# Four indirect gathers in flight instead of two, in the attention layer of a fused four-layer GNN kernel

## The reference

```python
h_in  = _attention_aggregate(h_proj, src, dst, a_in, n)
h_out = _attention_aggregate(h_proj, dst, src, a_out, n)
# inside, for each edge and each of 4 heads:
e = leaky_relu(score(sender) + score(receiver)); e_max = segment_max(e, receiver)
alpha = exp(e - e_max[receiver]); alpha = alpha / (segment_sum(alpha)[receiver] + 1e-8)
return segment_sum(h_proj[sender] * alpha, receiver)
```

## Time and profile before

| | us |
|---|---|
| median of 3 runs | 3679.42 (3669.36 to 3679.49) |
| the profiled execution | 3675.2 |
| its span, first to last instruction | 3673.1 |
| mean granted TensorE clock | 0.786 of full speed |

### The profile page before, as it was taken

The page is one execution under the profiler, slowest core; times in us unless marked ns, Lnnn a source line. Parts: engine busy times, 40 slices in busy tenths (PEclk is TensorE's granted clock), DMA queues, the critical chain, the costliest instruction groups (busy, mean ns, idle before and its releaser), DMA issues.

```text
span 3673.1 us, 46525 instructions
## 1 busy us (share of the span) xinstructions
PE 2217.1 (60%) x12603; PEld 1303.9 (35%) x12659; DVE 2275.1 (62%) x3122; ACT 834.8 (23%) x1389; POOL 1652.6 (45%) x1455
## 2 busy tenths in 40 slices
PE   0688777778968999857333333334557554336663
PEld 0333545544534555524311111112456211115563
DVE  8999888885497003532233334337577896349877
ACT  0198333320012001120000100002334221004442
POOL 7300333330477777740266666657644666630000
PEclk9799999999979999979555555555589897555797
DMA  2000111114434342044433333332367333320352
GB/s 65 0 0 0 45 45 45 45 40 135 125 108 117 87 100 42 1 96 102 67 90 89 91 93 90 90 86 74 88 206 232 101 88 96 88 48 0 107 176 85
DMA packets 195114, 301.51 MB, mean 82 GB/s; under 512 B 120540, under 2 KB 133818, under 8 KB 194922
## 3 DMA queue, kind: packets, MB, share of 16 engines
q1 hardware_dynamic: 138986, 175.88, 15.1%
q0 software_dynamic: 40512, 62.87, 9.2%
q10 hardware_dynamic: 15552, 61.94, 5.6%
HBM read 191.65 MB, written 88.01 MB: 76 GB/s over the span
## 4 chain that ended last, share of the span: by engine, by line
PE 28%; DMA 24%; issue 17%; DVE 15%; POOL 9%; ACT 5%; ACTq 0%; DVEq 0%; SPq 0%; POOLq 0%; PEldq 0%
DMA arena<-T_att,idx 23%; PE PS L537 10%; POOL arena L1304 9%; PE PS L698 6%; PE PS L883 6%; ACT arena L513 3%; DVE arena L558 3%; PE PS L972 3%; DVE arena L1195 1%; DVE arena L373 1%; PE PS L475 1%; DVE arena L489 1%; PE PS L959 1%; DMA T_att<-parts 0%; DVE arena L566 0%
## 5 line engine op out<-in xcount | busy, mean ns | idle before, releaser
L1304 POOL DMA_INDIRECT arena<-T_att,idx x864 | 843.2, 976 | 627.8 <-DMA arena<-T_att,idx 457.5
L537 PE MATMUL PS<-arena 128*128 128x400 f16 (+2 forms) x4320 | 781.0, 331 | 266.1 <-issue 106.0
L1139 DVE TENSOR_REDUCE arena<-PS 128x1024 f32 (+1 forms) x432 | 504.7, 1216 | 582.5 <-PE PS L1106 562.3
L537 PEld LDWEIGHTS PS<-arena 128*128 128x128 f16 (+2 forms) x4320 | 528.3, 158 | 509.1 <-issue 350.0
L1477 POOL DMA_INDIRECT order<-arena x400 | 513.3, 1283 | 252.4 <-issue 252.4
L1095 PE MATMUL PS<-ident_b,score_buf 128*32 128x128 bf16 x864 | 96.2, 279 | 552.9 <-ACT score_buf L1068 542.0
L1106 PE MATMUL PS<-arena,pick 128*128 128x512 bf16 x812 | 340.5, 525 | 139.7 <-DVE arena L1139 107.1
L558 DVE TENSOR_SCALAR arena<-arena 128x1600 f16<-128x1600 f16 x448 | 381.1, 896 | 59.8 <-PE PS L537 55.6
L698 PE MATMUL PS<-arena 128*128 128x512 f16 (+1 forms) x1575 | 318.7, 362 | 95.5 <-issue 82.1
L632 POOL TENSOR_TENSOR rdeg<-rdeg,arena 128x1600 f32<-128x1600 f32 x48 | 160.1, 3337 | 307.0 <-ACT arena L616 307.0
L1095 PEld LDWEIGHTS PS<-ident_b,score_buf 128*32 128x32 bf16 x864 | 71.3, 124 | 625.3 <-issue 554.7
(11 more groups left out here) (258 smaller groups left out, 2797.6 us busy)
## 6 DMA issues: line engine op xcount, KB each, us to landing
spill<-arena SPq DMA_DIRECT2D x108, 560.0 KB
arena<-spill ACTq DMA_DIRECT2D x108, 560.0 KB
arena<-A SPq DMA_DIRECT2D x50, 800.0 KB
A<-arena SPq DMA_DIRECT2D x50, 400.0 KB, 2.4
arena<-A SPq DMA_DIRECT2D x50, 400.0 KB
arena<-T_att,idx POOLq DMA_INDIRECT x864
order<-arena POOLq DMA_INDIRECT x400
T_att<-h SPq DMA_DIRECT2D x2, 1600.0 KB, 13.9
```

The source lines that it names most:

```text
L537: return t.matmul(where, lhsT, rhs, start=False, stop=True, skip_group_check=True)
L1139: v.tensor_reduce(cmax[d][:, u:u + 2, bass.ds(i * SLOTS + half * GROUP + q // 2 * QUAD, QUAD)], PS[:, u * BANK:(u + 2) * BANK].rearrange(" ...
L1304: p.indirect_dma_start(out=ring1[:, b, j, :], out_offset=None, in_=T_att[d][:, :], in_offset=bass.IndirectOffsetOnAxis(ap=idx[:, d, k:k + ...
```

## The change

`FLYING` goes from 2 to 4, and each of the three buffers of `ring1` gets four landing semaphores instead of two. `PER`, the number of gathers of a group that share a semaphore, becomes 2 instead of 4. A gather then waits for the gather four places before it, where it waited for the one two places before. The keep and the spill wait for four semaphores where they waited for two. The number of gathers, their order, sizes and buffers stay as they are.

```diff
-        landed1 = [[sem(f"landed1_{b}_{q}") for q in range(2)] for b in range(RING1)]
+        landed1 = [[sem(f"landed1_{b}_{q}") for q in range(4)] for b in range(RING1)]
...
-        FLYING = 2
+        FLYING = 4
         PER = GROUP // FLYING
```

## The result

The changed kernel takes 3375.75 us (median of 4, 3372.55 to 3378.3) beside 3679.45 for the kernel before: a ratio of 0.9184, 95% interval 0.917 to 0.9199. The forecast was 3436, its low end 3405. The way it moved was forecast rightly, and so was the mechanism in POOL's stream; the gain was 60 us larger than forecast.

The account below looks back on a forecast made before the run. POOL's gathers, waiting for landings, were taken to bound top 0 and the end of top 1. Saving 110 us in top 0, losing 10 in guard 0 and weighted 0, saving 143 in top 1 gave 243 less: 3436 us, range 3405 to 3540.

Parts of the forecast that it names:

- 1.25 us between gathers, landings well inside four places: POOL's stream: gathers start 1.25 us apart; a landing's 2.84 us fits within four starts, 5.0 us.
- The step across the keep, 1.75 us: POOL, between groups: one step of 1.75 us beside seven of 1.25, making 10.5 us a group.
- The two additions of 0.20: POOL, per group: 0.13 us for pauses without a releaser, 0.07 for late landings beside spills, giving 10.7 us.
- The first 36 us of guard 0: Start of guard 0, during DVE's whole-row casts: more in flight doesn't help, 12 gathers as before.
- The rest of guard 0, 157 us: Guard 0 after its first 36 us: 153 us plus 4 for more gather groups disturbing it, 112 gathers.
- Weighted 0, +6 us, a gather each 1.63: Weighted 0: 6 us longer, 194 us, from a third more gathers; 119 gathers at 1.63 us each.
- What ends top 1: End of top 1: the later of DVE's reduces (3049) and the gathers (3045), so DVE at 3049, against 3291.8.
- The lower bound, 3405: Whole kernel: 10.5 us a group, no loss in guard 0 or weighted 0 gives 3414; clock luck, 3405.
- Rival 1: Gather stream: landings slow down when more are in flight; half the gain a group, 3533 us; chance 0.14.
- Rival 2: Gather queue: gathers don't overlap, one finishes every 1.6 us; within 10 us of 3679; chance 0.04.
- Rival 3: DMA rings: gathers delay the spill, so POOL waits for the third buffer; 3759 us; chance 0.04.
- Rival 4: Guard 0: the 3 us lost per gather group double, 40 us on the path, about 3476; chance 0.06.

Follow-up runs that it names:

- e13: The kernel before the change (two in flight), unaltered, run again for a trace of its own: 3665.55 us.
- e4: Changed kernel, but POOL issues no gather from group 54 on until weighted 0 and its output are done: 4082.77 us.
- e2: Changed kernel with a small memset on POOL after each gather, so most gathers start 1.41 us apart: 3729.47 us.
- e7: Changed kernel with four gathers in flight in direction 0 but only two in direction 1: 3615.07 us, ratio 0.9876.
- e5: Changed kernel unaltered, run again in a later set: 4087.44 us, ratio 1.1177 to the kernel before.
- e12: Changed kernel unaltered, run once more in another set: 3361.67 us, ratio 0.9202 to the kernel before.
- e10: Changed kernel with SP's spill waiting for POOL's keep instead of the four landings: 3365.99 us, ratio 0.9213.

## Why the prediction was wrong, point by point

- **1.25 us between gathers, landings well inside four places:** right. 229.1 us of POOL's 323.1 idle are now "issue".
- **The step across the keep, 1.75 us:** a mis-sized term. It measured 1.38, so a group is 7 x 1.25 + 1.38 = 10.13, where the text had 10.5. The 0.53 us of idle time behind the cast were read as the price of a keep. With four in flight they are 0.16, so the rest probably was an unmarked wait for the landing two places back (in e13, again two in flight, it is 0.49 to 0.63 in a quiet stretch). The two additions of 0.20 came to 0.12: 556 us for 434 gathers is 10.25 a group. Over 54 groups the 0.45 that the forecast had too much is 24 us. Top 0 itself: 577 forecast, 564 measured, its gathers starting 4.5 us later than in before (1813.1 for 1808.6).
- **The first 36 us of guard 0:** right, 14 gathers for 12.
- **The rest of guard 0, 157 us:** the larger of the two mis-sized terms, 102.7 measured. The text took the 40 us over guard 1's length for a property of the stream ("the stage itself is disturbed by the stream") and carried it over. It was a property of the set of runs from which the trace came, as e13 shows for the kernel before: with the same two-deep stream beside it the stretch takes 103 us, and with no gathers at all (e4) the same 103. The size of 40 was too small besides: guard 1's 148 us for 56 groups make 137 for guard 0's 52, so 52 of the 189 us were unexplained, just what the measured stage is short of.
- **Weighted 0, +6 us, a gather each 1.63:** the stage came out at 188, unharmed, and a gather each 188 / 132 = 1.42, though the DMA engines were at 0.81.
- **What ends top 1:** the formula was right and the answer changed. DVE's side: 2696.2 + 277 = 2973. The gathers' side: last gather 2976.4 + 18 = 2994.4; measured 2994.34. Since guard 0 was so short, only 656 gathers were issued when top 1 began, for 674 forecast, and gathers ended the stage, not DVE.
- **After top 1:** right, nothing moved.
- **The lower bound, 3405:** it let guard 0 shrink by nothing below its 153 us, so it had no room for the larger of the two errors. (The 123 us that it saves in top 0 at 10.5 us a group should read 121: 431 x 10.5 / 8 = 566 for 687.)

By the same two formulas the miss splits. 3049 - 2994.3 = 55 us at the end of top 1. Had guard 0 kept its 157 us, DVE would have ended at 2696.2 + 54.3 + 277 = 3027.5, so some 33 us of the miss come with guard 0. Of the other 22, top 0 gives 16 (its end is at 2369 for 2385), by the gathers' pace, and weighted 0 gives 6. This split is worked out, not run. What is left of the 60 us lies outside the sum: the profiled execution ran 2 us over its median where the text had set it 4 under.

**Luck.** The sum has its sign from the pace of the gathers, and this was worked out. But the changed kernel ran in four sets, and was 8% faster in two and 12% slower in two. That the result fell in an undisturbed set was luck: nothing in the prediction foresaw the other kind, though its own trace came from it.

**The rivals.** Rival 1 (landings slower): no, 55.9 us of landing waits in all. Rival 2 (no overlap): no. Rival 3 (slower, spill and gathers block each other, 3759): its mechanism didn't occur, but a slower outcome did, 4087 to 4095 us, from a mechanism that no rival named: beside dense gathers PE's signals come late in a disturbed set. Rival 4 (guard 0 suffers more) is the nearest: it took the 3 us pauses as something that more gathers would double, and in a disturbed set they grew to 44 us. A better reading of the trace was to be had: the pauses ended with "remote" and with no work that could explain them, and a wait without an explanation deserves a rival with a larger price.

**What stays open.** What makes a set disturbed isn't known; it isn't the chip as a whole, nor the kernel's code or the waits on its landing semaphores, and whether it is the recording wasn't tested. Nor is it shown where PE's 1.40 us go, between the end of the instruction in its own record and the release of its reader. It is shown that the gathers' density decides whether it matters: e4 (gone once POOL stops), e2 (0.16 us more a gather, and 3729 us instead of 4087), e7 against e5. That two in flight do little harm because each blocked wait of POOL lets PE through is an inference, and e2 speaks against it in part: its pace is gained without a blocked wait on a landing. The same version in both kinds exists only for the changed kernel and the one before; what four-then-two takes undisturbed wasn't tried.

## What to carry to other kernels

Deepen a stream of gathers until no landing ends a wait (8% with four, 9% with no wait at all), and before a stage's length is carried into a forecast, explain it: a stage longer than its twin without the stream, with idle time that ends in no work of the kernel, may belong to the circumstances of the profile. Look first whether the profile has its landing times; where it lacks them for most transfers, take another one. And measure a change of this kind in several sets of runs: the deeper stream is 8% faster or 12% slower with the same program, and the only deeper version that gained in a disturbed one is four in flight first and two later (0.980 and 0.988, a gain of 2% and 1%).

## What was not expected of the hardware

- Four gathers in flight need no more time to land: 2.6 us median in the result and 2.5 in e12, and 2.6 for two in flight (e13). Only with SP's edit one trace of two has more, 3.0 (e10). (The Trainium skill, "DMA: Bandwidth & Descriptors", on the anatomy of a GpSimd DMA, gives 2.0 us plus bytes over 436 GB/s. That is an estimate of 2.2 us for 71.7 KB. The trace has 2.6 for these gathers of 128 rows.)
- In a disturbed set PE's results reach their readers at 1.40 us for each of its instructions (44.85 us for 32) while most gathers follow each other at 1.25 to 1.40 us, and ACT, DVE and PE itself all stand idle meanwhile. The edge is between two and three in flight. In the same traces most of the gathers' landing updates are missing (1660 of 13824 recorded in e5), and whether the recording is the cause is open.
- The kernel before hides this completely. Its end is set by gathers in both kinds (3665.55 in e13, 3675.2 in the profiled execution of before), while the rest of its guard 0 takes 103 or 153 us.
